# Windowed attention: one wait for each score product instead of one for each pair

## The reference, cut to what matters

```python
Q = (x @ Wq.T).reshape(B, S, HKV, G, HEAD_DIM)      # HKV = 4, G = 4, HEAD_DIM = 16
K = (x @ Wk.T).reshape(B, S, HKV, HEAD_DIM)
V = (x @ Wv.T).reshape(B, S, HKV, HEAD_DIM)
scores = jnp.einsum('bskgd,bswkd->bskgw', Q, K_win) * scale   # 257 keys around each query
scores = jnp.where(valid[None, :, None, None, :], scores, jnp.float32(-jnp.inf))
attn = jax.nn.softmax(scores, axis=-1)
out = jnp.einsum('bskgw,bswkd->bskgd', attn, V_win)
```

## Time and profile before

| what | value |
|---|---|
| median of 3 runs | 3204.3 us (3202.83 to 3207.18) |
| profiled execution, its own time | 3175.27 us |
| its span, first to last instruction | 3173.4 us |
| granted TensorE clock, mean | 0.989 |
| busy over the span: PE, DVE, ACT, POOL | 96%, 62%, 54%, 24% |
| the windowed attention, about | 1157 to 1681 us |

### The profile page before, as it was taken

The page is one execution under the profiler, slowest core; times in us unless marked ns, Lnnn a source line. Parts: engine busy times, 40 slices in busy tenths (PEclk is TensorE's granted clock), DMA queues, the critical chain, the costliest instruction groups (busy, mean ns, idle before and its releaser), DMA issues. The chain is left out here.

```text
span 3173.4 us, 49527 instructions
## 1 busy us (share of the span) xinstructions
PE 3053.4 (96%) x16616; PEld 1908.5 (60%) x16617; DVE 1954.9 (62%) x4607; ACT 1721.0 (54%) x3801; POOL 763.4 (24%) x1037
## 2 busy tenths in 40 slices
PE   8999998998999989999998999999999999998999
PEld 4455556558999963333334666665555666666555
DVE  6999995653333346666664787785333777777342
ACT  6776762213333326665665888875222777776221
POOL 1111113550000035555533222221011112112111
PEclk9999999999999999999999999999999999999999
DMA  9900004013111121111101000000001000000000
GB/s 330 318 1 1 1 1 165 29 54 103 46 48 48 45 77 29 31 29 26 29 14 42 10 11 9 10 8 32 1 0 36 9 11 10 9 9 5 14 14 27
DMA packets 114255, 134.11 MB, mean 42 GB/s; under 512 B 14478, under 2 KB 100342, under 8 KB 113786
## 3 DMA queue, kind: packets, MB, share of 16 engines
q1 hardware_dynamic: 106042, 109.54, 10.6%
q0 software_dynamic: 7872, 21.77, 2.2%
q10 hardware_dynamic: 128, 0.10, 0.0%
HBM read 60.30 MB, written 60.83 MB: 38 GB/s over the span
## 5 line engine op out<-in xcount | busy, mean ns | idle before, releaser
L1880 DVE CUSTOM_DVE_ANT_0 sb_win_masked<-ps_win_pss,sb_win_around 128x384 f32<-128x384 f32 (+1 forms) x512 | 256.3, 538 | 167.0 <-PE ps_win_pss L2008 166.9
L2320 ACT ACTIVATE sb_loc_pr<-ps_loc_psw,sb_loc_nb,sb_loc_sc 128x256 f32<-128x256 f32 x512 | 281.0, 569 | 135.9 <-DVE sb_loc_nb L2465 135.9
L2547 PE MATMUL ps_stk_banks<-sb_stk_w,sb_loc_hT 128*128 128x512 f32 x768 | 348.3, 603 | 2.7 <-ACT sb_loc_hT L2287 2.7
L1742 ACT ACTIVATE sb_win_pT<-ps_win_pst 128x512 f32<-128x512 f32 x368 | 199.8, 596 | 167.3 <-PE ps_win_pst L2019 167.2
L1473 PE MATMUL ps_exp_ps<-sb_exp_xT,sb_exp_here 128*128 128x128 f32 x2272 | 266.8, 276 | 0.0
L1473 PEld LDWEIGHTS ps_exp_ps<-sb_exp_xT,sb_exp_here 128*128 128x128 f32 x2272 | 261.0, 193 | 0.1
L2008 PE MATMUL ps_win_pss<-sb_win_kT,sb_win_q 32*128 32x384 f32 (+1 forms) x1024 | 230.4, 520 | 31.7 <-DVE sb_win_qtok L1880 21.3
L2547 PEld LDWEIGHTS ps_stk_banks<-sb_stk_w,sb_loc_hT 128*128 128x128 f32 x768 | 141.2, 190 | 177.9 <-issue 177.9
L752 PE MATMUL ps_rec_psp<-sb_rec_hT,sb_rec_w 128*128 128x512 f32 x512 | 230.1, 592 | 0.8 <-DVE sb_keep_modf L543 0.8
L2842 DVE SCALAR_TENSOR_TENSOR sb_mlp_hid<-ps_stk_banks,sb_stk_col,sb_mlp_gl 128x512 f32<-128x512 f32 (+1 forms) x112 | 75.1, 672 | 245.5 <-ACT sb_mlp_gl L2797 245.3
L2019 PE MATMUL ps_win_pst<-sb_win_qm,sb_win_kT 32*128 32x512 f32 x736 | 211.2, 647 | 1.5 <-ACT sb_win_pT L1742 1.5
(11 more groups left out here) (362 smaller groups left out, 6725.2 us busy)
## 6 DMA issues: line engine op xcount, KB each, us to landing
sorted_tokens<-sb_rec_blank SPq DMA_DIRECT2D x9, 4224.0 KB, 30.2
sb_exp_rows<-sorted_tokens SPq DMA_DIRECT2D x71, 128.0 KB, 2.0
expert_results<-sb_exp_res SPq DMA_DIRECT2D x71, 128.0 KB, 1.7
sb_moe_w_in<-in_L_ffn_w_in_eDF SPq DMA_DIRECT2D x8, 512.0 KB, 10.7
sb_moe_w_sw<-in_L_ffn_w_swiglu_eDF SPq DMA_DIRECT2D x8, 512.0 KB, 10.8
sb_exp_w_out<-in_L_ffn_w_out_eFD POOLq DMA_DIRECT2D x8, 512.0 KB, 8.7
sb_stk_angles<-in_angles SPq DMA_DIRECT2D x32, 128.0 KB, 3.8
sb_stk_xs_b<-sb_stk_y SPq DMA_DIRECT2D x64, 63.5 KB
```

What stands on the lines that cost most here:

```text
L1742: nc.scalar.activation(pT[:, n % PARTS], pst[:, n % TURNED], ACT.Exp, scale=SC).then_inc(s_e, 1)
L1880: nc.vector.tensor_tensor_reduce(masked[:, pair % 2, j, 0:keys], pss[:, (n + j) % PLAIN, 0:keys], around[:, first:first + keys], 1.0, -3e3 ...
L2320: e = nc.scalar.activation(pr[:, hf, h], psw[:, hf, h // 2, h % 2 * 256:h % 2 * 256 + 256], ACT.Exp, scale=sc8[:, b, hh:hh + 1], bias=nb[: ...
L2547: t = nc.tensor.matmul(psa[:, c], hT[:, b, k, 1 - k:P + 1 - k], w[:, k, c * 512:(c + 1) * 512], start=(k == 0), stop=(k == KD - 1))
```

## The change

Each plain product now waits for its own bank, right ahead of it, and so does each turned one. The functions that waited for the whole wave are gone. VectorE waits for one product ahead of each of the two maxima, and its self-wait now comes first. No arithmetic, tile or buffer changes, and neither does the order of the products.

```diff
@@ VectorE, maxima @@
-                    dve.wait_ge(s_s, n + 2)
                     first, pair = 0 if where(u)[1] else P, n // 2
                     if pair >= 2:
                         dve.wait_ge(s_top, 2 * (pair - 1))
                     for j in range(2):
+                        dve.wait_ge(s_s, n + j + 1)
                         nc.vector.tensor_tensor_reduce(masked[:, pair % 2, j, 0:keys], ...
@@ TensorE @@
-                def maxima_done(u, k):
-                    for j in range(2):
-                        n = u * AH + 2 * k + j
-                        if n >= PLAIN:
-                            pe.wait_ge(s_top, n - PLAIN + 1)
-
-                def exps_done(u, k):
-                    for j in range(2):
-                        n = groups_before(u) * 4 + 2 * k + j
-                        if n >= TURNED:
-                            pe.wait_ge(s_e, n - TURNED + 1)
@@ scores @@
                     n = u * AH + 2 * k + j
+                    if n >= PLAIN:
+                        pe.wait_ge(s_top, n - PLAIN + 1)
@@ scores_turned @@
                     n = groups_before(u) * 4 + 2 * k + j
+                    if n >= TURNED:
+                        pe.wait_ge(s_e, n - TURNED + 1)
@@ step @@
-                        if 0 <= s < NT:
-                            maxima_done(s, k)
-                        if turned:
-                            exps_done(s - 1, k - 2)
                         for j in range(2):
```

## The result

| | before | after |
|---|---|---|
| median, same chip | 3206.0 us (5 runs) | 3191.1 us (5 runs) |
| ratio | | 0.995, 95% interval 0.9935 to 0.9964 |
| profiled execution, span | 3173.4 us | 3190.8 us |
| granted clock in it | 0.989 | 0.982 |

The change makes the kernel 14.9 us faster, 0.5% (11.5 to 20.8 us by the interval); 5 us were forecast and 3191 was the range's lower end. The two profiled spans cannot be set against each other: the part of the kernel ahead of this stage took 1155 us in the one and 1183 in the other (first wave of the stage, from the span's start), with code that is the same, while the part from its last wave on took 1494 and 1496. So the stage is compared by itself. From its first to its last wave it took 523.7 us before and 511.7 after.

What follows compares the result with a forecast made beforehand. TensorE, VectorE and ScalarE were taken to wait for each other in turn. Savings of 0.09 + 0.06 = 0.15 us a unit over 32 units gave 4.8 us, taken as 5 off the median: 3199 us, range 3191 to 3207.

Steps and rivals of the forecast that it cites:

- The mechanism of the inner unit: Slot by slot in one unit: 0.09 us from slots 1 to 3, 0.06 in slot 6, together 0.15 us.
- the four signs: Expected in the trace: early first plain products, earlier maxima in mixed waves, projection still waiting for hT, unit 16.4 us.
- the projection's wait total would grow: Slot 3's projection still waits for ScalarE's modulated copy hT, and its wait total grows over 24.1 us.
- VectorE's half: First maximum no longer waits for the second product; its extra wait costs 0.05 us, ends 0 and 0.1.
- the late pair's release: Second plain and second turned product start 0.10 us after the event that frees them, 0.15 meaning no gain.
- 32 of them at that length would be 530 us, so it stands for the stage: One 16.56 us unit was taken for all 32 of the stage, so its gain was multiplied by 32.
- This costs nothing and by itself saves nothing: First plain and first turned product of a wave start when TensorE is ready; priced at no gain by itself.
- A: Rival: stalls go more fully, slot 3 held by TensorE alone; 0.3 us a unit, 10 us, 3194 us; chance 0.12.
- C: Rival: late products wait for the early pair's second passes; 0.37 us a unit slower, 12 us, 3216 us; chance 0.11.
- B: Rival: nothing moves, since the same event frees the late pair; 0 +- 2 us, 3204 us; chance 0.15.

Runs made afterwards that it cites:

- tensor_only: The kernel before with only TensorE waiting product by product and VectorE still waiting for pairs; ratio to the kernel before 0.995 (0.9937 to 0.9964).
- copy_between: The changed kernel with ScalarE's modulated copy in slot 2 moved between the two exponentials; ratio to the kernel before 0.9948 (0.9932 to 0.9963).
- score_first: The changed kernel with VectorE's score wait written ahead of its self-wait; ratio to the kernel before 0.9929 (0.9902 to 0.9956), on another chip 0.9947.
- rep_after_2: The changed kernel unchanged, timed again against the kernel before on the same chip; ratio 0.9963 (0.9949 to 0.9977).
- turned_only: The kernel before with only TensorE's turned products waiting one by one, plain banks awaited by the whole wave, VectorE by pairs; single run 3208.4 us.
- rep_before: The kernel before, unchanged, run once more for its trace; single run 3175.3 us, stage 519.2 us.
- plain_only: The kernel before with only TensorE's plain products waiting one by one, turned banks awaited by the whole wave, VectorE by pairs; single run 3199.7 us.

## Why the prediction was wrong

**The mechanism of the inner unit held, in slot 1 by luck.** The late product of slot 1 came at 1.68, as forecast, but out of two misses that cancel: the first maximum started 1.06 after its product instead of 1.02, and the late product followed the end of the accumulator's read by 0.06 instead of 0.10. Slot 2 came at 3.51 (forecast 3.52), slot 3's late turned product at 5.33 (5.38), the projection at 6.51 (6.51), held by ScalarE as said and with nothing recovered of the 0.45 us stall but what ScalarE handed on. The projection still follows the first exponential by 1.83. Two of the four signs were off in part. Slot 6's plain products start 0.02 apart and not 0.2 to 0.4; the forecast's own numbers had it so, with TensorE ready at 1.67 and the late plain product at 1.68. And the forecast that the projection's wait total would grow was off as a reading: the profile now puts 7.5 us of it down to ScalarE and 18.2 to "issue", 25.7 together against 24.1.

**VectorE's half** had the right sign in the sum and too low a price: 1.06 after the product where I took 1.02, 0.12 us for the second wait where I took 0.05 with an end at 0.1. It is a loss, and the order of two lines would have avoided it.

**One term was mis-sized: the late pair's release.** "I take 0.10, with 0.15 as the other end" measured 0.05 (1396.86 to 1396.91; in slot 6, 1402.91 + 0.60 = 1403.51 to 1403.56). I had put the best case at the nearest row and left nothing below it. That is 0.04 to 0.05 us in slot 6. A unit gains 0.10 up to slot 4 and 0.10 in slot 6, with the roundings 0.21 and not 0.15.

**The step that failed was "32 of them at that length would be 530 us, so it stands for the stage".** The stage had 524 us, and the 6 us between the two were the sign that some units are of another shape. The sum booked the 11 units that are not inner ones at 0.15 each, 1.7 us; they give 4.7 of the 9.1. The 21 inner ones give 4.4, close to the sum that I had for all. What makes them different goes back to what the prediction said of the early pair: "This costs nothing and by itself saves nothing". It holds where side work fills slot 1. In unit 18 the early turned product let ScalarE begin 1.11 us sooner and the projection start 0.49 us sooner. Why the last two units give 0.69 us each is not shown slot by slot.

**The clock was no term at all, and what lies beyond the stage is open.** The measured 14.9 us are 5.8 more than the 9.1 at the full clock (2.4 to 11.7 more, by the interval). The table of stretches had shown 0.97 for 1420 to 1480 us, and I did not ask why. Filling the idle time of three units of the kernel before took the half clock out of them in three traces of three, where five of seven with bunched plain waits have it, and gave 0.14% (0.03 to 0.25%). By chance alone three clean traces would come 2 times in 100, taking 5 of 7 as the rate, and 6 times in 100 with the 3 of 5 of the kernel before itself. That the idle time brings it is made likely, not certain, and unit 1 is not explained.

It is also a small sum. In its five traces the half clock of units 17 and 18 cost the kernel before 1.6, 0, 2.8, 0 and 2.8 us, 1.4 on average. Over all traces the stage takes 521.3 us before (five) and 511.6 after (three), 9.6 less. That lies within the second timed comparison, 11.8 (7.3 to 16.2), and below the first, 14.9 (11.5 to 20.8). The rest of the first one is in no trace of the stage. The mean granted clock of the timed runs was higher than that of the kernel before on the same chip in four of the five later comparisons of a kernel with separate plain waits (tensor_only 0.9885 to 0.9866, copy_between 0.9833 to 0.9801, score_first 0.9840 to 0.9801 and 0.9882 to 0.9868) and level in the fifth (rep_after_2, 0.9870 to 0.9868). But only one run of each set is traced, and in the traces the code ahead of the stage, which is the same in all, scatters between 0.97 and 0.98 by itself. So whether the change brings the clock there or chance does is not shown.

**The rivals.** A's time, 3194, lies nearest to what was measured, but not for its reason: slot 3 was not released to TensorE alone. C is refuted: in slot 3 the late pair starts 0.20 and 0.33 after the early one, before the early plain product's second pass at 0.43, and in slot 6 0.02 and 0.15 after; no slot waited for second passes. B is out by the unit's length.

What stays open: the part of the first comparison's gain that no trace of the stage shows, and score_first's 0.9929, 23 us where its stage explains 13; whether the half clock in unit 1 has the same cause as that in units 17 and 18; and what holds turned_only's first turned product.

## What to carry to other kernels

Before a unit's gain is multiplied, list the units of another shape and work one of them out: where filler work is missing, an early start reaches the next engine, and here such units gained 0.5 to 0.7 us instead of 0.21. When a wait is split, find what ends last for each of the waiters; here splitting the wait on the maxima paid and splitting the other alone cost. Of two waits ahead of one instruction try both orders; here the one that is met last had to be written first.

## What the runs showed of the hardware

- A product on one 32-row group started up to 0.33 us after its partners on other groups (1396.58 and 1396.91) without delaying them or itself: the second pass comes 0.53 us after the first in both turned products, as before the change.
- The order of two waits was worth 0.12 us on VectorE (0.94 against 1.06 from product to maximum). With its own wait right ahead of it TensorE's late turned product started 0.05 us after the end of the exponential that released it; with all waits of the wave bunched ahead the wave started 0.14 after it.
- Idle time of 0.71 to 0.78 us ahead of slot 2, in the two neighbouring units 17 and 18, went with TensorE's clock at half for 3.4 to 6.8 us in a unit in five of seven traces and made the unit 1.6 to 3.4 us longer than in rep_before. With transposes of no use in that gap none of three traces had it, and the kernel was 0.14% (0.03 to 0.25%) faster. In unit 1 the half clock came about as often with 0.3 us of idle time in the record (three of eight traces, plain_only's 1.2 us among them) as with 2.1 to 2.3 (three of seven).
